# Block of eight groups of a transformer layer computed from attention outputs^T and sums times x^T, with block weights centred

## The reference, cut to what matters

```python
qkv = x @ w_attn + b_attn                      # x (2, 4096, 256)
attn = softmax(q @ k.T / 16 + causal mask)
x1 = layernorm(x + (attn @ v) @ w_proj + b_proj)
scores = x1 @ w_router                         # the best 3072 of 4096 rows are selected
y = x1, with x1[i] replaced by gelu(x1[i] @ w_block) for the selected rows i
out = layernorm(x1 + y)
```

## Time and profile before

| | us |
|---|---|
| median of 3 runs | 969.58 |
| lowest and highest | 966.6, 970.15 |
| the profiled execution's own time | 969.85 |
| its span, first to last instruction | 968.1 |
| PE busy | 940.7 (97%) |
| DVE busy | 769.6 (79%) |
| ACT busy | 635.2 (66%) |
| POOL busy | 274.3 (28%) |

### The profile page before, as it was taken

The page is one execution under the profiler, slowest core; times in us unless marked ns, Lnnn a source line. Parts: engine busy times, 40 slices in busy tenths (PEclk is TensorE's granted clock), DMA queues, the critical chain, the costliest instruction groups (busy, mean ns, idle before and its releaser), DMA issues.

```text
span 968.1 us, 15640 instructions
## 1 busy us (share of the span) xinstructions
PE 940.7 (97%) x5078; PEld 806.6 (83%) x5078; DVE 769.6 (79%) x1473; ACT 635.2 (66%) x993; POOL 274.3 (28%) x436
## 2 busy tenths in 40 slices
PE   9999999999999999999999999999999999998992
PEld 7889988888888888888888988888888888887771
DVE  4688996967966785789779989887899778568877
ACT  3566675764864585478555875686688558447985
POOL 3523124253042034513214253323203302111162
PEclk9999999999999999999999999999999999999996
DMA  6535344444253344567432533435777534336934
GB/s 190 175 123 171 110 142 121 121 130 141 76 164 104 104 151 158 165 213 228 153 126 82 186 111 108 164 94 180 241 237 251 172 100 131 119 100 219 314 131 174
DMA packets 85282, 149.53 MB, mean 154 GB/s; under 512 B 7761, under 2 KB 17618, under 8 KB 85202
## 3 DMA queue, kind: packets, MB, share of 16 engines
q1 hardware_dynamic: 85202, 148.54, 48.5%
HBM read 108.66 MB, written 39.85 MB: 153 GB/s over the span
## 4 chain that ended last, share of the span: by engine, by line
PE 93%; DVE 4%; issue 1%; ACT 1%; POOL 0%; ACTq 0%; DVEq 0%; POOLq 0%
PE sbank L514 37%; PE fbank L514 13%; PE obank L1048 11%; PE obank L1050 11%; PE obank L1049 11%; PE obank L1042 2%; PE obank L1044 2%; PE obank L1043 2%; PE fbank L1339 1%; PE fbank L1138 1%; PE mbank L946 1%; PE mbank L969 1%; DVE cmp L1502 1%; PE obank L554 1%; DVE tail L1751 0%
## 5 line engine op out<-in xcount | busy, mean ns | idle before, releaser
L514 PE MATMUL sbank<-qT,xT 128*128 128x512 f32 (+2 forms) x1728 | 413.2, 379 | 0.0
L514 PEld LDWEIGHTS sbank<-qT,xT 128*128 128x128 f32 x1728 | 306.4, 189 | 53.0 <-issue 0.3
L871 ACT COPY ring<-sbank 128x512 f32<-128x512 f32 (+3 forms) x288 | 157.5, 549 | 176.7 <-PE sbank L514 125.3
L1000 DVE TENSOR_TENSOR ring_lo<-ring,parts 128x1024 fp32r<-128x1024 f32 (+4 forms) x176 | 181.6, 1039 | 33.2 <-ACT parts L995 32.4
L1048 PE MATMUL obank<-ring_lo,vs 128*128 128x512 f32 x480 | 184.1, 384 | 4.1 <-ACT ot_sb L1107 1.6
L1050 PE MATMUL obank<-parts,vs 128*128 128x512 f32 x480 | 182.6, 380 | 0.0
L1049 PE MATMUL obank<-parts,vs 128*128 128x512 f32 x480 | 182.3, 380 | 0.0
L995 ACT CAST parts<-ring 128x1024 fp32r<-128x1024 f32 (+4 forms) x176 | 145.9, 834 | 52.4 <-PE obank L1050 39.7
L981 DVE TENSOR_TENSOR ring<-ring,mbank 128x1024 f32<-128x1024 f32 (+4 forms) x176 | 159.4, 946 | 9.4 <-PE mbank L969 9.4
L988 ACT ACTIVATE ring<-ring 128x1024 f32<-128x1024 f32 (+4 forms) x176 | 143.9, 845 | 24.7 <-DVE ring L981 24.4
L913 DVE TENSOR_TENSOR runmax<-ring,runmax 128x1024 f32<-128x1024 f32 x84 | 106.2, 1264 | 64.7 <-ACT ring L871 64.0
(11 more groups left out here) (222 smaller groups left out, 1204.7 us busy)
## 6 DMA issues: line engine op xcount, KB each, us to landing
vs<-v_scratch SPq DMA_DIRECT2D x288, 256.0 KB, 2.8
v_scratch<-vnew SPq DMA_DIRECT2D x30, 512.0 KB, 3.3
xres<-x SPq DMA_DIRECT2D x16, 512.0 KB, 4.7
out<-tail SPq DMA_DIRECT2D x32, 256.0 KB, 3.0
x_scratch<-xres SPq DMA_DIRECT2D x14, 512.0 KB, 3.1
y_scratch<-yb SPq DMA_DIRECT2D x14, 512.0 KB, 4.6
tail<-x_scratch SPq DMA_DIRECT2D x28, 256.0 KB, 3.5
tail<-y_scratch SPq DMA_DIRECT2D x28, 256.0 KB, 4.3
```

What stands on the lines that cost most here:

```text
L514: mm = eng.matmul(o, lhs(lh, k), rhs(rh, k), start=n == 0, stop=n == len(todo) - 1)
L871: act.copy(slot(n)[:, c0:], sbank[n % NSS][:, c0:]).then_inc(a_copy, 1)
L1000: dve.tensor_tensor(slots_lo(ns, c0), slots(ns, c0), f32(hi_of(u)), ALU.subtract).then_inc(v_lo, 1)
```

## The change

It touches the block of the turned groups below `LATE`: `upright(G)` is true for groups 3 to 7 and 11 to 13, eight in all. With h = outputs / sum + x + b and layer norm x1 = rs * (h - mean), the product x1 @ W equals (rs / sum) * (outputs + (x + b) * sum) @ Wc, where Wc are the weights minus the mean of each column. So the left factor is built transposed, from `ot_sb`, the row of sums spread over the partitions, and x^T, which lies in DRAM.

```diff
+    upright = lambda G: not straight(G) and G < LATE
+    block_fills = lambda G: [f for j in range(2) for f in ([] if upright(G) else [("ft", G, j)]) + [("ff", G, j)]]
...
+            def block_sums(pe):
+                pe.wait_ge(ld_ffw, 32)
+                pe.wait_ge(g_const, 2)
+                for k in range(CC):
+                    mm = pe.matmul(w_sums, ones[:, :], wb[:, k, :], start=k == 0, stop=k == CC - 1)
+                mm.then_inc(p_wsum, 1)
-            pe_fill["values weights"] += [lambda pe, m=m: query_sums(pe, m) for m in range(CC)] + [bias_product, bias]
+            pe_fill["values weights"] += [lambda pe, m=m: query_sums(pe, m) for m in range(CC)] + [bias_product, bias, block_sums]
             def block_parts(dve):
                 dve.wait_ge(ld_ffw, 32)
+                dve.wait_ge(p_wsum, 1)
+                dve.scalar_tensor_tensor(out=wb, in0=w_sums[:, None, :].broadcast_to([P, CC, C]), scalar=-1.0 / C, in1=wb,
+                                         op0=ALU.mult, op1=ALU.add).then_inc(v_wb, 1)
...
+            def bias_store(sp):
+                sp.wait_ge(v_btot, 2)
+                sp.dma_start(b_dram.rearrange("(a c) -> a c", a=1), b_tot[0:1, :]).then_inc(st_b, 16)
+            def bias_load(sp):
+                sp.wait_ge(st_b, 16)
+                sp.wait_ge(v_wdiff, 1)
+                for k in range(CC):
+                    sp.dma_start(b_cols[:, k:k + 1], b_dram[k * P:(k + 1) * P].rearrange("(p a) -> p a", a=1)).then_inc(ld_bc, 16)
...
+                        pe.wait_ge(v_wb, 1)
...
-                    filled(sp, ("ft", G - 2, 1))
+                    if not upright(G - 2):
+                        filled(sp, ("ft", G - 2, 1))
...
+                if uprights(G):
+                    dve.wait_ge(g_fs, uprights(G))
...
+                if upright(G):
+                    pool.wait_ge(v_rs, 2 * (G + 1))
+                    if upright(G - 2):
+                        pool.wait_ge(a_gelu, 2 * (G - 1))
+                    pool.tensor_tensor(fscale[:, G % 2], rs, rsum[:, :], ALU.mult).then_inc(g_fs, 1)
...
+            def sums_store(sp):
+                sp.wait_ge(a_ot, CC * (turned(G) + 1))
+                sp.dma_start(s_dram[G:G + 1, :], ot_sb[P - 1:P, CC - 1, :]).then_inc(st_s, 16)
+            def sums_load(sp):
+                sp.wait_ge(st_s, 16 * (nth + 1))
+                sp.wait_ge(st_y, 16 * G)
+                sp.dma_start(sums_wide, s_dram[G:G + 1, :].broadcast_to([P, GQ])).then_inc(ld_s, 16)
+            def rows_load(sp, c):
+                sp.wait_ge(st_y, 16 * G)
+                if c:
+                    sp.wait_ge(g_rt, CC * nth + c)
+                sp.dma_start(rows_wide, xt_rows[b][:, c, g * GQ:(g + 1) * GQ]).then_inc(ld_xr, 16)
+            def rows_scale(dve, c):
+                dve.wait_ge(ld_xr, 16 * (CC * nth + c + 1))
+                dve.wait_ge(ld_s, 16 * (nth + 1))
+                dve.scalar_tensor_tensor(out=rows_wide, in0=rows_wide, scalar=b_cols[:, c:c + 1], in1=sums_wide, op0=ALU.add,
+                                         op1=ALU.mult).then_inc(v_sx, 1)
+            def rows_add(pool, c):
+                pool.wait_ge(v_sx, CC * nth + c + 1)
+                filled(pool, ("o", G, 1))
+                pool.tensor_tensor(ot_sb[:, c, :], ot_sb[:, c, :], rows_wide, ALU.add).then_inc(g_rt, 1)
+            def up_fhi(act, j):
+                act.wait_ge(g_rt, CC * (nth + 1))
+                act.copy(up_hi(j), ot_sb[:, :, 2 * j * P:2 * (j + 1) * P]).then_inc(a_fhi, 1)
+            def up_flo(dve, j):
+                dve.wait_ge(a_fhi, 2 * G + j + 1)
+                dve.tensor_tensor(up_lo(j), ot_sb[:, :, 2 * j * P:2 * (j + 1) * P], f32(up_hi(j)),
+                                  ALU.subtract).then_inc(v_flo, 1)
+            def up_block(pe, j):
+                pe.wait_ge(v_flo, 2 * G + j + 1)
+                freed(pe, ("ff", G, j))
+                for t in range(2):
+                    mm = split3(pe, bank_of(("ff", G, j))[:, t * C:(t + 1) * C],
+                                lambda h, k: (up_lo if h else up_hi)(j)[:, k, t * P:(t + 1) * P],
+                                lambda h, k: WB[:, h, k, :], CC)
+                mm.then_inc(p_out, 1)
+            def up_gelu(act):
+                act.wait_ge(g_fs, nth + 1)
+                for j in range(2):
+                    filled(act, ("ff", G, j))
+                    for t in range(2):
+                        op = act.activation(y_pair(G, j)[:, t], bank_of(("ff", G, j))[:, t * C:(t + 1) * C],
+                                            ACT.Gelu_apprx_tanh, scale=fscale[:, G % 2, 2 * j + t:2 * j + t + 1])
+                    op.then_inc(a_gelu, 1)
```

More of the change, by code:

```diff
@@ L308, in program @@
     straight = lambda G: groups[G][1] < STRAIGHT
+    upright = lambda G: not straight(G) and G < LATE
+    uprights = lambda G: sum(upright(H) for H in range(G))
     turned = lambda G: sum(not straight(H) for H in range(G))
     out_fills = []
-    block_fills = lambda G: [("ft", G, 0), ("ff", G, 0), ("ft", G, 1), ("ff", G, 1)]
+    block_fills = lambda G: [f for j in range(2) for f in ([] if upright(G) else [("ft", G, j)]) + [("ff", G, j)]]
     for G, (b, g) in enumerate(groups):
@@ L350, in program @@
         v_dram = nc.dram_tensor("v_scratch", (B, NT, P, 2, C), F32, kind="Internal").ap()
+        s_dram = nc.dram_tensor("s_scratch", (B * NG, GQ), F32, kind="Internal").ap()
+        b_dram = nc.dram_tensor("b_scratch", (C,), F32, kind="Internal").ap()
         with nc.sbuf_tensor("xT", [P, 2, CC, T], F32R) as xT_:
@@ L385, in program @@
         b_tot = sb("b_tot", [P, C])
+        fscale = sb("fscale", [P, 2, QT])
         wr = sb("wr", [P, C])
@@ L450, in program @@
         v_ot = sem("v_ot")
+        p_wsum, st_b, ld_bc = sem("p_wsum"), sem("st_b"), sem("ld_bc")
+        st_s, ld_s, ld_xr, v_sx, g_rt, g_fs = (sem("st_s"), sem("ld_s"), sem("ld_xr"), sem("v_sx"), sem("g_rt"),
+                                               sem("g_fs"))
         a_ot, g_xres, v_rs, v_h, v_bn, v_mv = (sem("a_ot"), sem("g_xres"), sem("v_rs"), sem("v_h"), sem("v_bn"),
@@ L535, in program @@
         x1p_of = lambda G, j: x1p if G < LATE else late_x[:, G - LATE, j]
+        b_cols = w_col
+        sums_wide, rows_wide = (yb[:, 2 * n:2 * n + 2].rearrange("p t c -> p (t c)") for n in range(2))
+        up_hi = lambda j: vnew_b[:, j]
+        up_lo = lambda j: x1p[:, :, 2 * j * P:2 * (j + 1) * P]
+        w_sums = obank[0][:, C:2 * C]
         left_out = mbank[:, 0:NT]
@@ L703, in prepare @@
             at("dve", "prepare bias", bias_total)
+            def bias_store(sp):
[6 more added lines that the diff above has]
+                    sp.dma_start(b_cols[:, k:k + 1], b_dram[k * P:(k + 1) * P].rearrange("(p a) -> p a", a=1)).then_inc(ld_bc, 16)
+            at("sp", "bias columns", bias_store)
+            at("sp", "bias columns", bias_load)
             for op in (block_parts, router_sum):
@@ L869, in copy @@
                 elif n >= STAGED:
-                    act.wait_ge(v_wb, 2)
+                    act.wait_ge(v_wb, 3)
                 act.copy(slot(n)[:, c0:], sbank[n % NSS][:, c0:]).then_inc(a_copy, 1)
@@ new lines, in rows_scale @@
+            def rows_scale(dve, c):
+                dve.wait_ge(ld_xr, 16 * (CC * nth + c + 1))
+                dve.wait_ge(ld_s, 16 * (nth + 1))
+                if not nth and not c:
+                    dve.wait_ge(ld_bc, 16 * CC)
+                dve.scalar_tensor_tensor(out=rows_wide, in0=rows_wide, scalar=b_cols[:, c:c + 1], in1=sums_wide, op0=ALU.add,
[4 more added lines that the diff above has]
+                pool.tensor_tensor(ot_sb[:, c, :], ot_sb[:, c, :], rows_wide, ALU.add).then_inc(g_rt, 1)
@@ L1368, in pe_f @@
                     if G == 0:
-                        pe.wait_ge(v_wb, 2)
+                        pe.wait_ge(v_wb, 3)
                     freed(pe, ("ff", G, j))
@@ L1399, in add @@
                 pool.wait_ge(a_gelu, 2 * G + j + 1)
+                if upright(G):
+                    pool.wait_ge(a_x1, QT * G + 2 * j + 2)
                 if late:
@@ L1414, in aggr @@
                     dve.bn_aggr(mv_y[:, b, g * QT + t, :], bnst[:, 1, t, :]).then_inc(v_mvy, 1)
-            for j in range(2):
+            if upright(G):
+                at("sp", "ffn sums", sums_store)
+                at("sp", "ffn sums", sums_load)
+                for c in range(CC):
+                    at("sp", "ffn rows", lambda sp, c=c: rows_load(sp, c))
+                    at("dve", "ffn scale", lambda dve, c=c: rows_scale(dve, c))
+                    at("pool", "ffn rows", lambda pool, c=c: rows_add(pool, c))
+                for j in range(2):
+                    at("act", "ffn fhi", lambda act, j=j: up_fhi(act, j))
+                    at("dve", "ffn flo", lambda dve, j=j: up_flo(dve, j))
+                    pe_fill[("ff", G, j)] = lambda pe, j=j: up_block(pe, j)
+                    at("pool", "ffn add", lambda pool, j=j: add(pool, j))
```

(4 more changed lines are left out.)

4 lines of the change are left out of this document (3 added, 1 removed).

## The result

The changed kernel takes 972.0 us, the median of 12 runs (969.54 to 974.41); the kernel before, in 12 runs beside it, takes 967.95 (965.75 to 970.65). The ratio is 1.0041, with a 95% interval from 1.0028 to 1.0055. That is 4 us slower where the forecast was 6 us faster: the forecast missed by about 10 us, and the time lies inside the range from 958.5 to 973.

A forecast was written before the change was run, and what follows sets the result against it. It took PE as the bound: 968.1 - 7.5 (transposes) + 0.5 (sums) + 1.0 (chain lateness) = 962.1 us of span, 963.6 as a median against 969.58 (-0.6%); 8-in-10 range 958.5 to 973.

The forecast's parts named there:

- PE as the bound: From first scores to 900 us, time is the sum of PE's work; PE is busy 940.7 of 968.1 us.
- The transposes: On PE, eight groups lose two batches of four transposes: 0.47 us a batch, 7.5 us less, ends 5.8 and 9.6.
- The added sums: On PE at the start, two float32 matmuls of 256 columns for the weights' column sums add 0.5 us.
- The added work: In eight groups DVE gets 11 us, POOL 24, ACT 6, all beside PE's work; 0 for PE.
- the planner can place the products as before: Block products in eight groups: the shorter chain lets them keep their places; lateness from its DMA costs 1.0 us in all.
- some 10 us: Length of the block's new chain, additions, row load, scale, high and low parts, in place of 18.7 us.
- ACT's cover: ACT's 333 idle us hide the gelu's added 0.8 us a group, 6 us in all, beside PE's work.
- Rival 1: At the block products: chain 3.5 us later than planned, 2.4 covered, PE idles 1 us a block; 970 us, 20%.
- Rival 2: DVE waits for a DMA and collides with POOL, 5.6 us a group, so PE idles; 979 us, 17%.
- Rival 3: Products no longer tied to norm; new orders remove PE waits of 1.6 and 0.8 us; 960 us, 12%.
- a margin for the new orders: Allowance, without its own size, in the 8-in-10 range from 958.5 to 973 us, beside rivals 1 and 3.
- the closing 68 us get longer: Listed sign of a wrong prediction: the last groups and the search, taken as unchanged, would take longer.

The follow-up runs named there:

- table A: 12 numbers of the planner's tables changed: on the changed kernel 962.1 us, ratio 0.9942; 11 of them on the kernel before 970.65 us, 1.0020.
- narrow rows: Changed kernel, orders kept, rows scaled on DVE and added on POOL over 16 of 512 columns only: 970.67 us, ratio 1.0033.
- one number: Changed kernel with the planner's preference for PE's scores set from 0 to 4, from 840 us of PE's planned time on: 968.12 us, ratio 1.0003.
- gelu ahead: The kernel of "one number" with block 13's gelu moved ahead of group 15's first exponential on ACT: 973.46 us, ratio 1.0067.
- six products of ones: Changed kernel, orders kept, with six more matmuls of ones on PE ahead of group 14's late block product: 973.73 us, ratio 1.0045.
- table A from 840 us on: Changed kernel planned with old tables until 840 us of PE's planned time and with table A's 12 numbers behind it: 966.43 us, ratio 0.9977.

## Why the prediction was wrong, point by point

**PE as the bound and "an edit counts by what it takes from PE": right,** with the orders kept (0.9955), and in the account of the changed kernel up to 874 us (4.3 us ahead, with 6.5 us less of work on PE in the whole kernel). What the forecast had no term for is PE's clock: waits in other places came with more time at half clock, 1.8 us in the profiles and up to 5.3 in the medians.

**The transposes: about right.** 7.5 us were forecast from starts. The run with 48 left out gives 6.5 (5.0 to 7.8) for all 64, and PE's work fell by 6.5 us with the added sums in it. That the 0.11 us behind a batch is the price of a weight load was inferred; the rows show only that it stays as long as one transpose is left. **The added sums: under-sized.** The two products are four matmuls in the trace, not two, and the four take 0.8 us from start to start (15.70 to 16.48), 1.1 busy; 0.5 were forecast, since the eight of L625 come from four products.

**The added work: right.** By the run without it DVE and POOL cost 0.8 us, not told from nothing. Their durations were a little longer than taken: `rows_add` 1.63 against 1.40, `rows_scale` 0.79 against 0.69, the low parts 0.82 against 0.69. The Trainium skill ("SBUF — State Buffer", section "Who interferes with whom") says that a DVE instruction with two SBUF inputs contends with a GpSimd one that reads SBUF, and that the later of two contenders "fully blocks". If each of the 32 instructions had been held, DVE would have lost an estimated 33 us. The rows show 0.1 us a scale and 0.14 a low part on the average, and the run without this work shows that the end didn't feel it.

**The failed step: "the planner can place the products as before".** The chain of the block is shorter than the one it replaces, as said, though not "some 10 us": in block 13 it is 15.0 us from the turn to the first product, in place of 21.9, and its second low part ends at 867.7 us in place of 875.9. But the planner doesn't put an operation where it was; it puts it where it can start. Block 13's products became ready ahead of the last maxima, took 2.9 us there, and the gelu behind them took 4.1 us of ACT with its two table loads, ahead of the one exponential that PE needed. An operation that comes early pushed back the operation that was late. In the profile 3.3 us went at group 15 and 2.7 in the closing part, and a gain of 4.3 us became a loss of 1.7; the medians say 4. The run with the gelu moved ahead shows the price of its place. How the rest of the 4 us divides between orders and clock stays open.

**ACT's cover.** "ACT 333 idle us, +6 us lies beside PE's work" was true of the sum and not of the place. At the start of a group's values PE has only what is left of the group before; there the chain is maxima, subtraction, exponential, high part, low part, and ACT is on it. I had read the stretch from 840 to 900 only for DVE's spare time.

**The rivals.** Rival 1 gave nearly the right size (970) by another mechanism, so that is luck: the list of PE's waits has no wait for the new low parts (`up_flo`). Its sum is wrong too: the parts that it names make 4.1 us, not 3.5, and would have given 976. Rival 2 is refuted. Rival 3, new orders with 2.4 us of gain, names the right cause with the wrong sign: the planner's orders put the changed kernel anywhere from 7.1 us faster to 4 us slower than the kernel before. The range had "a margin for the new orders" without a price; a rival "new orders cost 4 us and more", worked out from a group's start, was missing. The sign that I had listed, "the closing 68 us get longer", came true: behind group 15's values they are 2.7 us longer. That 972.0 us lies in the range from 958.5 to 973 is owed to this margin and to rival 1, not to the sum.

**Is the change worth it?** With orders that suit it, yes: 0.9926 and 0.9942 against a kernel before that table A makes slower. That is 5.6 to 7.1 us, near the 6.5 us that left PE. But the changed kernel was given new tables and the kernel before only table A, so what the change gives with the best orders of each isn't known.

## What to carry to other kernels

Where a planner writes the orders, a change of the operations is two changes, and the second can be larger than the first: 12.6 us here for one and the same missing work, about half of it idle time of PE and half its clock in the two profiles. Price them apart, by a run with the orders kept, and retune the tables before judging the change. When a chain gets shorter, ask what its end will now stand ahead of, above all on an engine that has to load a table for it, and look for it where PE has least work in hand: at the start of a group and at the end of the program.

## What the runs showed of the hardware

Short idle times of PE came with stretches of about 3.4 us at half clock in the middle of the kernel, as shown in the section on the result. In the changed kernel one begins right behind a wait of 2.0 us (until 419.98), another at the end of a wait of 4.4 us (until 881.64). In the run planned anew without the 48 transposes one lasted 10.2 us (877.0 to 887.2); it began during a wait of 3.5 us.

At the half level (1.2 GHz) the starts of the matmuls of 512 columns lie 0.43 us apart, not 0.23, so a stretch costs about 1.6 us on top of the wait. The same wait doesn't always bring one. The wait of 2.0 us at 420 us is there in several runs with the changed kernel's orders up to that point; the clock fell behind it in four of them (the changed kernel, narrow rows, one number, gelu ahead) and stayed at its full level in two (six products of ones, table A from 840 us on). Waits of 1.6 us before and with one number were not followed by one at once, but the next ones, of 1.4 us and 6 us later, were. Filling PE with six products didn't prevent a later one, so what brings it on stays open. Executions of one kernel differ by it as well: the 12 of the changed kernel range from a mean clock of 0.988 (969.54 us) to 0.980 (973.41 us), and the longest, 974.41 us, had 0.982.

A change of ACT's table cost 1.28 us with nothing beside it: in the run with the gelu ahead the load starts at 875.96, the moment the gelu ends (875.95), and the exponential starts at 877.26. The Trainium skill ("ScalarE: Activation LUTs", section "What ACT_TABLE_LOAD costs") gives the same 1283 ns and adds a drain of about 1380 ns to every switch; these rows show no such drain.
